# Attention on context rows as loaded, split products in both layers, new orders of work on all engines, in a graph attention and mixture of experts kernel

## The reference

```python
x = x + xattn(ctx, layernorm(x))     # 4 graphs, 512 nodes; two GAT layers, 8 heads x 64
x = x + moe(layernorm(x))            # 2048 rows: router, 32 experts of which 4, shared MLP

def gat_layer(x, adj, W, a_self, a_neigh, b):      # "adj" is layernorm(x), not 0 and 1
    feat = einsum('nf,hfo->hno', x, W)
    e = leaky_relu(attn_self[:, :, None] + attn_neigh[:, None, :]) + (-1e10) * (1 - adj)
    out = softmax(e) @ feat + b
    return elu(out)                                # heads side by side: [512, 512]
# moe: scores = sigmoid(x @ router_w.T); best 3 of 8 groups, best 4 of their experts;
# 80 slots per expert; out[tok] += w * (silu(X G_e) * (X U_e)) D_e; plus
# shared = silu(x @ sg.T) * (x @ su.T) @ sd.T      # inner width 512, every row
```

## Time and profile before

| what | value |
|---|---|
| median of 3 runs | 539.58 us (537.31 to 541.82) |
| profiled execution, its span | 534.8 us |
| PE busy, share of the span | 439.8 us, 82% |
| DVE, ACT, POOL busy | 270.0, 159.8, 127.0 us |
| DMA moved | 85.55 MB, mean 160 GB/s |

### The profile page before, as it was taken

The page is one execution under the profiler, slowest core; times in us unless marked ns, Lnnn a source line. Parts: engine busy times, 40 slices in busy tenths (PEclk is TensorE's granted clock), DMA queues, the critical chain, the costliest instruction groups (busy, mean ns, idle before and its releaser), DMA issues.

```text
span 534.8 us, 6440 instructions
## 1 busy us (share of the span) xinstructions
PE 439.8 (82%) x2363; PEld 339.8 (64%) x2363; DVE 270.0 (50%) x670; ACT 159.8 (30%) x275; POOL 127.0 (24%) x118
## 2 busy tenths in 40 slices
PE   0251687789958898997999999999999999999920
PEld 0221343334445576876789898888988898888810
DVE  5853638988975999667132243322334334332300
ACT  0222422433187301111112242333324233333220
POOL 0577200300000100000321233332234344332211
PEclk9997679999978999999975999999999999999985
DMA  8687060110126500000178977899979897977250
GB/s 260 162 178 208 25 237 0 79 78 1 80 81 237 198 10 11 0 2 0 39 135 258 277 212 235 249 286 288 319 225 321 256 303 241 307 249 224 28 91 12
DMA packets 41057, 85.55 MB, mean 160 GB/s; under 512 B 14496, under 2 KB 14496, under 8 KB 39488
## 3 DMA queue, kind: packets, MB, share of 16 engines
q1 hardware_dynamic: 32208, 67.74, 37.7%
q0 software_dynamic: 6720, 16.07, 15.1%
q10 hardware_dynamic: 2096, 1.31, 0.8%
HBM read 67.01 MB, written 18.10 MB: 159 GB/s over the span
## 4 chain that ended last, share of the span: by engine, by line
PE 64%; DVE 16%; DMA 7%; issue 5%; ACT 4%; POOL 2%; another core or an unknown queue 1%; ACTq 0%; DVEq 0%; POOLq 0%
PE bank L1266 21%; PE bank L1156 11%; PE bank L1158 10%; PE bank L1157 10%; PE bank L1214 7%; PE bank L1151 4%; DVE bn L846 2%; DMA out_dram<-room 1%; DMA room<-rows_dram,tok 1%; DMA ix<-idx_dram,ixg 1%; DVE xs L905 1%; DMA ctx_buf<-in_ctx_dram,ix 1%; DVE e1r L904 1%; DMA xs<-in_x_dram 1%
## 5 line engine op out<-in xcount | busy, mean ns | idle before, releaser
L1266 PE MATMUL bank<-e1r,ring 128*128 128x80 f32 x1024 | 126.1, 284 | 1.1 <-DVE th L1075 1.1
L1266 PEld LDWEIGHTS bank<-e1r,ring 128*128 128x128 f32 x1024 | 124.9, 202 | 1.3 <-DVE th L1075 1.2
L654 POOL DMA_INDIRECT out_dram<-ctx_buf,tok x32 | 49.2, 1538 | 150.8 <-DMA out_dram<-ctx_buf,tok 73.7
L1075 DVE TENSOR_TENSOR th<-th,bank 128x160 f32<-128x160 f32 (+1 forms) x48 | 21.3, 443 | 125.7 <-ACT th L785 104.6
L1082 DVE TENSOR_TENSOR down<-ring,down 128x1024 fp32r<-128x1024 f32 x32 | 39.2, 1225 | 54.7 <-ACT down L762 54.4
L785 ACT ACTIVATE th<-bank 128x160 f32<-128x160 f32 (+1 forms) x48 | 19.3, 403 | 158.0 <-PE bank L1158 79.5
L1214 PE MATMUL bank<-w,h1T 128*128 128x512 f32 x128 | 58.8, 617 | 5.5 <-DVE sg L899 3.4
L624 POOL DMA_INDIRECT room<-rows_dram,tok x32 | 32.6, 1017 | 90.5 <-ACT tok L672 81.0
L1214 PEld LDWEIGHTS bank<-w,h1T 128*128 128x128 f32 x128 | 24.8, 197 | 37.7 <-issue 29.8
L762 ACT ACTIVATE down<-ring 128x1024 fp32r<-128x1024 f32 x32 | 33.8, 1057 | 32.6 <-PE bank L1158 30.3
L1151 PE MATMUL bank<-ident,ring 128*128 128x128 f32 x48 | 8.5, 336 | 26.9 <-DMA ring<-n_L_ffn_shared_gate_dram 13.0
(11 more groups left out here) (171 smaller groups left out, 728.3 us busy)
## 6 DMA issues: line engine op xcount, KB each, us to landing
ring<-in_L_ffn_W_gate_dram SPq DMA_DIRECT2D x32, 512.0 KB
ring<-in_L_ffn_W_up_dram SPq DMA_DIRECT2D x32, 512.0 KB
ring<-in_L_ffn_W_down_dram SPq DMA_DIRECT2D x32, 512.0 KB
xs<-in_x_dram SPq DMA_DIRECT2D x4, 1024.0 KB, 6.1
out_dram<-xs SPq DMA_DIRECT2D x4, 1024.0 KB, 3.9
out_dram<-room POOLq DMA_DIRECT2D x4, 1024.0 KB, 8.3
rows_dram<-ctx_buf SPq DMA_DIRECT2D x2, 1024.0 KB, 5.3
rows_dram<-h1T SPq DMA_DIRECT2D x2, 1024.0 KB, 4.9
```

Source lines behind the costliest of these rows:

```text
L654: pool.indirect_dma_start(out=out_rows, out_offset=bass.IndirectOffsetOnAxis(ap=tok[:, n:n + 1], axis=0), in_=ey[:, n % 3, :], in_offset=N ...
L1075: v.tensor_tensor(h, h, up, ALU.mult).then_inc(gu_free, 1)
L1266: last = pe.matmul(bank[2 + i % 2][:, at:at + CAP], w[:, c, P * k:P * k + P], xgT[:, e % 3, c, :], start=(c == 0), stop=(c == KC - 1))
```

## The change

- **Attention without a gather ahead of it.** The context is loaded in the order it has in DRAM and both layers run on it. `f2`, the result of layer two plus one, is stored to `att_dram[g]`. POOL adds its rows to `xs` by an indirect DMA with `ix2` that accumulates (`add_attention`). The minus one comes from a constant row of ones, `normed` and the bias of the D output (`minus_one`).
- **Split products in both layers.** `w0`, `w1`, the transposed context and `h1T` get high and low parts. The bias of layer two is a thirteenth matmul with `ones` and `b1row`. The loads of W0 and all of W1 (256-byte pieces) stand at the head of ACT's queue; POOL makes the low part of W1.
- **Another ELU.** Layer one: ACT `Relu(-z)`, `Exp(-.)`, DVE `max(z + 1, .)`, ACT the high part, DVE the low part. Layer two: ACT Exp, DVE `max(min(., 1), z)`.
- **Check.** Its spread comes from 16 `Square` on ACT with a sum instead of `bn_stats` on DVE.
- **Routing.** `max`, `match_replace` and `is_equal` instead of `max_index`, casts and comparisons with an iota.
- **Orders.** PE, ACT and DVE get orders written out call by call. Four S units, their Silus on ACT between the router's Tanhs, stand inside the row stage; between the three list steps there are fewer units than before. The rest of the shared units is spread over 29 experts instead of 32.
- **Buffers.** Weight ring 5 instead of 3, rows gathered 4 ahead in 5 buffers instead of 5 in 7, `ey` 2 instead of 3, `ob` one graph instead of two.

```diff
-RING = 3
-XRING = 7
-AHEAD = 5
+RING = 5
+XRING = 5
+AHEAD = 4
+EYS = 2
@@ ACT queue
-            act.dma_start(w0[:, :].rearrange("f (h o) -> f h o", h=HEADS),
+            act.dma_start(b0c[:, :], b0.rearrange("h o -> (h o)").rearrange("(c p) -> p c", p=P),
...
+            for c in range(KC):
+                act.dma_start(w_raw[:, c, :].rearrange("f (h o) -> f h o", h=HEADS),
+                              W1[:, P * c:P * c + P, :].rearrange("h f o -> f h o")).then_inc(ld_w1, 16)
@@ start of ACT
+            ctx_high(0)
+            ctx_high(1)
+            for t in range(TPG):
+                square(t)
+            act.wait_ge(ld_w1, 16 * KC)
+            for c in range(KC):
+                act.activation(wts[:, HIGH, c, :], w_raw[:, c, :], ACT.Copy).then_inc(w_high, 1)
+            below(0)
+            below(1)
+            exponent(0)
...
@@ layer two on PE
+            def second_layer(n):
...
+                pe.matmul(b[:, :], ones[:, :], b1row[:, :], start=True, stop=False)
+                for c in range(KC):
+                    last = product(b[:, :], lambda h: h1T[g % 2][:, h, c, P * t:P * t + P], lambda h: wts[:, h, c, :],
+                                   start=False, stop=(c == KC - 1))
+                last.then_inc(l2_full, 1)
@@ POOL
+            def add_attention(g):
+                pool.wait_ge(idx2_ready[g], 16 * TPG)
+                pool.wait_ge(ones_stored, 16 * GRAPHS)
+                for t in range(TPG):
+                    pool.wait_ge(f2_stored[t], 16 * (g + 1))
+                for t in range(TPG * g, TPG * g + TPG):
+                    pool.indirect_dma_start(
+                        out=xs[:, t, :], out_offset=None, in_=att_dram[g],
+                        in_offset=bass.IndirectOffsetOnAxis(ap=ix2[:, t:t + 1], axis=0),
+                        compute_op=ALU.add).then_inc(x1_ready[g], 16)
...
+            unless_one_hot(pool, slow_pool)
+            add_attention(0)
+            add_attention(1)
+            add_attention(2)
+            power(0)
+            power(1)
+            add_attention(3)
+            power(2)
+            power(3)
@@ units
-            while shared_rest and spent + weight[shared_rest[0][0]] <= total * (e + 1) / EXPERTS:
+            while shared_rest and spent + weight[shared_rest[0][0]] <= total * (e + 1) / (EXPERTS - 3):
@@ PE, row stage and lists
+            rows_in(0)
+            router(0)
+            rows_in(1)
+            shared_hidden(0)
+            router(1)
+            rows_in(2)
+            logits_out(0)
+            logits_out(1)
+            shared_hidden(1)
+            router(2)
+            rows_in(3)
+            shared_hidden(2)
+            router(3)
+            logits_out(2)
+            logits_out(3)
+            shared_hidden(3)
+            shared_hidden(4)
+            for n in range(TPG):
+                shared_out(n)
+            selected()
+            shared_hidden(5)
+            shared_hidden(6)
+            merged()
+            shared_hidden(7)
+            tokens()
+            for n in range(TPG, 2 * TPG):
+                shared_out(n)
+            shared_hidden(8)
+            spread(0)
```

More of the change, by code:

```diff
@@ new lines, in _ @@
+            act.wait_ge(tp_full, GROUP["CS"] + 1)
+            act.activation(sums[:, :, :], bank[GROUP["CS"] % 2][:, 0:4 * KC].rearrange("p (b n two) -> p b n two", b=2, two=2)[:, :, :, 0],
+                           ACT.Copy).then_inc(tp_free, 1)
+            below(10)
+            hidden_high(8)
+            below(11)
+            hidden_high(9)
+            second(5)
+            exponent(10)
+            exponent(11)
+            ctx_high(3)
+            for t in range(10, 13):
+                square(t)
@@ L765, in _ @@
+            evac(GROUP["TOK"], tok[:, :], EXPERTS, parts=CAP)
+            for n in range(TPG, 2 * TPG):
+                output(("D", n))
+            silu(("S", 8))
+            shared_high(("S", 8))
+            split_down(0)
+            spread(0)
+            for u in mixed_part:
                 kind, n = u
@@ new lines, in _ @@
+            largest_ctx(0)
+            for t in range(TPG):
+                largest(t)
+            largest_ctx(1)
+            v.wait_ge(w_high, 1)
+            v.tensor_tensor(w0(LOW), w_raw[:, KC, :], w0(HIGH).bitcast(f32), ALU.subtract).then_inc(w0_low, 1)
+            ctx_low(0)
+            ctx_low(1)
+            prepare_bias()
+            place(0)
+            place(1)
+            above(0)
+            above(1)
+            place(2)
+            hidden_low(0)
+            hidden_low(1)
@@ L1128, in _ @@
                                    ALU.subtract).then_inc(tok_ready, 1)
-            for u in early:
-                hidden(u)
+            gated(("S", 8))
+            split(("S", 8), high=False)
             low_down(0)
@@ new lines, in merged, with tokens @@
+            def merged():
+                n = GROUP["MERGE"]
+                b = bank[n % 2]
+                bank_free(n)
+                pe.wait_ge(kk1_ready, 1)
+                for g in range(GRAPHS):
+                    last = pe.matmul(b[0:EXPERTS, CAP * g:CAP * g + CAP], ident[:, EXPERTS * g:EXPERTS * g + EXPERTS],
+                                     kk1[:, :], start=True, stop=True)
+                last.then_inc(tp_full, 1)
+            def tokens():
+                pe.wait_ge(tok_ready, 1)
+                group(GROUP["TOK"], [(lambda b: b[0:CAP, 0:EXPERTS], tokf[:, :])])
```

1474 lines of the change are left out of this document (856 added, 618 removed).

## The result

The changed kernel takes 546.4 us (median of 4 runs, 545.5 to 547.9) where the kernel before takes 540.0: a ratio of 1.012 with a 95% interval of 1.008 to 1.015. It is slower by about 1%, where I had forecast 508 us. Timed together once more, the two stood at 1.014 (1.008 to 1.020), and the changed kernel took 546.0 us. All ratios are of undisturbed runs (in the first timing of the kernel with all four edits only two of six), so they can stand a little off the ratio of the medians. So where a gain is given in microseconds against the changed kernel, the two were mostly not timed together, and a difference of 2 or 3 us is not clear of noise.

What follows compares the result with a forecast made beforehand. PE was taken to bound the units by its own time, PE and DVE layer two, a gather wait the start. Layer two's end 112 + 376 + tail 15 = 503 us, plus 4.8 for runs over profile: 508; range 487 to 532.

Steps and rivals of the forecast that it cites:

- PE full after that: Sign for the expert units: from the experts' beginning near 247 us PE stays full; a window under 95% proves it wrong.
- 241 us of units: Experts and remaining shared units: 234.5 us of PE work, 2.6 at the last output and 4 for the clock.
- Start, 38 forecast: Start: without the gather ahead of the layers, layer two begins at 38 us instead of 72, bounds 29 and 56.
- I take 24: Start: ACT's wait for all of W1 ends at 24 us, between bounds of 15 and 42.
- ACT comes to it at 15 us: Start, low bound: W1 is never waited for and ACT reaches it at 15 us, after W0 at 9.2.
- Row stage, 82 forecast: From E, layer two's end (forecast 112 us), to the selection: 82 us, 63 of matmuls and 19 of PE idle.
- Lists, 53 forecast: Selection to the experts' beginning at E+135: 53 us, with PE idle twice for 9 us between the list steps.
- Clock, 4 us of 0 to 8.5: Turn to experts: 1.2 GHz from 274 to 291 us cost 8.5 us before; 4 put for the new order.
- Tail, 15 forecast: From PE's end to the span's end: 15 us instead of 21, a gain of 6.1 us.
- so its 7.84 us are hidden under PE: Tail: the last shared output comes three experts earlier, so its addition's 7.84 us no longer count.
- rival (3): ACT between Tanhs and Silus: seven table loads instead of one, 7.7 us more, time 513 (521 by the skill page); chance 0.06.
- The additions (4): Units: chained expert additions, 5.95 us each, become the bound; slower from 7.8 us each, 574 at longest landing; chance 0.10.

Runs made afterwards that it cites:

- all four edits: Changed kernel with start loads reordered, lists filled with shared units, gathers five ahead and two row stage orders turned round: 500.4 us, ratio 0.944 timed with the three-edit kernel.
- The orders alone: Changed kernel with POOL's `power(0)` ahead of `add_attention(2)` and DVE's graph 3 statistics ahead of S0's product: 539.8 us, ratio 1.003.
- the unused matmuls: Changed kernel plus 34 matmuls with unused results ahead of `merged()` and 34 ahead of `tokens()`: 543.9 us, ratio 1.003.
- the first two experiments: Changed kernel with the next gather issued ahead of the shared addition: 538.9 us; changed kernel with gathers five ahead in the same five buffers: 539.7 us.

## Why the prediction was wrong

Most mechanisms of the gain were there (not that of the tail). The step that failed most is "PE full after that" with its 241 us of units: I left out the places where the new orders make an engine pause, and what the clock does behind each.

- **Start, 38 forecast, 44.6 measured.** The failing term is W1: "I take 24". ACT's wait for it ended at 32.2, which is 8.2 us more, and the rest of the way took 12.4 us for my 13.9. My low bound failed too: "ACT comes to it at 15 us". W0 landed at 9.4, but ACT was still issuing W1's loads until 23.6, which I had priced at nothing, and came to W1 at 29.6. With other loads out of the way layer two starts at 31.2 us (28.3 with all four edits, just under my low bound of 29), and the kernel is 15 us faster.
- **Layer two, 74 forecast, 72.6 measured.** Right. The low parts on POOL took 1.27 us each, inside my bounds, and hidden.
- **Row stage, 82 forecast, 88.4 measured.** Graph 0's normalisation began at E+4 as forecast, and PE had its first rows at E+4.9, the end of a wait of 4.82 us. But its transposes ran at half clock, and DVE's low parts were done at 128.9 us, E+11.7 for my E+8.5. Graph 3's scales came at E+34 for my E+29, since DVE's statistics of graph 3 stood behind a wait of 4.91 us for ACT. `power(0)` stood behind four indirect issues of 1.54 us, 2.4 us long; I had looked at POOL's queue only for `power(1)`. The orders alone give 5.3 of the 6.4 us back.
- **Lists, 53 forecast, 59.8 measured; two idle stretches of 9 us forecast, 8.6 and 9.0 measured.** The pauses were right to half a microsecond, and their price was wrong: I counted their length, not the clock behind them. To the experts' first transposes it took 3.2 us more than forecast, about what the unused matmuls gave back (2.8). The other 3.6 lie between these transposes and the first expert matmul, 2.5 of them a wait, and were not in my sum. Filling both pauses gives 19 us behind the selection: their lengths less the remainder of 3.8 are 13.8; the other 5 I put down to the clock, in the lists and in the first units, by subtraction only.
- **Units, 241 with the clock forecast, 265.0 measured.** "PE full after that" failed. The sign that I had named, a window with PE under 95%, is there at 380 us (4.30 of 10). I wrote that the ring of five helps nothing and did not price the gather depth, which went from five to four. The stalls are 9.3 us; the half clock behind those at 380 and 507 us is two units at 7 in place of 3.7 and the matmuls just behind each (eleven shared ones, six outputs), some 10 us together. In the kernel before, the depth alone costs 8.5 us.
- **Clock, 4 us of 0 to 8.5.** Too little: the same turn to the experts held half clock from 265 to 281 us, half of 16 us. That is 4 us more than I had put, and with the 9.3 and the 10 it makes up nearly all of the 24 us by which the units came out longer.
- **Tail, 15 forecast, 14.5 measured, for the wrong reason.** The failing step is "so its 7.84 us are hidden under PE". A bare unit (5.40 us) gives back only half a microsecond over an addition (4.87 us), so the 8 us are not hidden. In the kernel before, the spread alone gained nothing. The changed kernel's tail is short only because PE is late: the stall and the half clock at 507 to 520 us let the chain catch up. Once the stalls were mended the tail was 20 us again (20.3 in the runs of the first two experiments), and where they were left, 14 to 16.
- **Rivals.** Table loads: one load in all behind the layers, at 143.0 us, though Tanhs and Silus alternate behind it; rival (3) fell. The additions (4) cost 4.87 us in the quiet tail and 5.95 was my figure; they don't bound the units (POOL waited 140.6 us for ACT at L689 and 21.7 for another addition, and their median landing was 4.3 us where the earlier trace rows have 5.2), but they bound the end once PE is early. A single landing took 7.8 us. Slower had 0.10 and happened by none of my mechanisms.

Do the terms add? Of the 42 us between forecast and span, the four edits give 46 (546.0 to 500.4, timed together). By the ratios it is 37 to 53 (from 1.012 to 0.944, and from 1.014 to 0.916), since the kernel before varied; so the sum is good to several microseconds at best. They don't mend the tail, and the start gains more than I had forecast. What stays open: how much of the stall's price is the gather standing in the queue behind the 1 MB addition and how much the addition's own slower landing among the experts (7.8 us in the tail; there the next addition waited another 11.5 and 11.9 us for it). Open too is why the clock falls at the turn to the experts, and how W1's lateness splits between issue and landing. Shared additions in smaller pieces were not tried.

## What to carry to other kernels

A pause of TensorE is not priced by its length alone: look at the granted clock of the windows behind it. When a change takes a buffer or a depth of prefetch away, find the rarest, longest item in that queue and ask whether the depth covers it, since the median lands in time and the stall comes from the other. And when a stage is freed, follow the second chain to the end: here TensorE gained 14 us and the serial additions kept 6 of them.

## What the hardware showed that I had not expected

- Issuing a load in small pieces can hold the issuing engine: four loads of 256 KB took 21.8 us of ACT's time with 8 MB of other loads beside them (DMA share 1.0 and more from 8 to 28 us, 343 to 411 GB/s), 9.7 us with 1.5 MB beside them.
- After TensorE stood 5.70 us, its granted clock was at 1.2 GHz for 11 us though it was busy throughout; after 2.79 us too, for some 9. After the 2.5 us at the first expert it was, for some 15, even where TensorE had been kept at work until then.
- Tanh and Silu alternated on ScalarE with one table load (1.28 us) between the first of each. The Trainium skill (ScalarE: Activation LUTs, What ACT_TABLE_LOAD costs) says that every switch to a different table set costs a load of about 1283 ns. The load here took as long; but by this trace, once it was done before the first Silu, neither Tanh nor Silu needed another.
- An indirect accumulating DMA of 128 rows into SBUF takes 1.54 us to issue and 7.0 to 8.6 to land.
